# One first stage for a four-layer attention kernel on one Trainium2 core: loads, normalisation and weight folding of layer 0 merged

## The reference, cut to what matters

```
x = x + tanh(g_xattn[0]) * L0_xattn(layernorm(x), ctx, Wq, Wkv_expand, Wout)
# L0_xattn: 16 heads of 16; qp = q @ Wq.T ; k, v = split(ctx @ Wkv.T)
# scores = (qh . kh) / 4, causal, softmax, out = attn . vh, out @ Wout.T
x = x + tanh(g_ffn[0])   * L0_ffn(layernorm(x), ...)          # experts
...
```

## Time and profile before

| what | us |
|---|---|
| median of three runs (lowest, highest) | 2333.84 (2321.99, 2335.94) |
| the profiled execution's own time | 2323.12 |
| its span, first to last instruction | 2321.3 |
| stages load, norma0, fold0: start to first product of q0 | 45.78 |
| q0, its products | 27.09 |
| PE busy over the span | 2176.7 (94%) |
| DVE / ACT / POOL busy | 1479.5 / 923.5 / 1095.1 |
| mean granted TensorE clock | 0.961 |

### The profile page before, as it was taken

One profiled execution on the slowest core, in us unless ns is written; L12 is line 12 of the kernel. 1 busy time (PEld: TensorE's weight loads), 2 busy tenths in 40 slices (PEclk: granted clock), 3 DMA queues, 4 the chain that ended last, 5 costly groups with the idle time before them and its releaser, 6 DMA issues. The chain is left out here.

```text
span 2321.3 us, 38613 instructions
## 1 busy us (share of the span) xinstructions
PE 2176.7 (94%) x13750; PEld 1552.8 (67%) x13750; DVE 1479.5 (64%) x2519; ACT 923.5 (40%) x1430; POOL 1095.1 (47%) x618
## 2 busy tenths in 40 slices
PE   6768999899999998999999999898999999998998
PEld 4447998666665657666666665787565566667997
DVE  2775444477777757787777775413777777744444
ACT  1442444434444452212444444112344444424443
POOL 0330333037777770464777777001077777722332
PEclk7878999999999999999999999899999999998999
DMA  4472732375564513225545552295855545303332
GB/s 84 123 249 94 226 113 90 91 188 111 114 134 105 132 40 127 57 84 127 126 100 137 117 119 49 74 339 226 233 114 123 119 102 133 83 9 111 117 117 83
DMA packets 122054, 285.59 MB, mean 123 GB/s; under 512 B 31355, under 2 KB 73903, under 8 KB 118172
## 3 DMA queue, kind: packets, MB, share of 16 engines
q1 hardware_dynamic: 121244, 281.95, 45.7%
q0 software_dynamic: 672, 1.84, 0.2%
HBM read 237.15 MB, written 46.41 MB: 122 GB/s over the span
## 5 line engine op out<-in xcount | busy, mean ns | idle before, releaser
L1314 DVE TENSOR_REDUCE keep_top<-banks 128x1 f32<-128x500 f32 x945 | 595.6, 674 | 218.5 <-PE banks L1221 218.3
L1391 ACT ACTIVATE att_ex<-banks 125x896 f32<-125x896 f32 x576 | 501.0, 918 | 230.0 <-PE banks L1214 229.9
L1247 PE MATMUL banks<-att_ex,att_v 125*64 125x448 f32 x2304 | 464.7, 545 | 0.0
L1446 POOL TENSOR_TENSOR att_acc<-att_acc,att_ex 125x896 f32<-125x896 f32 x186 | 391.8, 2106 | 68.0 <-ACT att_ex L1391 54.2
L1221 PE MATMUL banks<-keep_kh,keep_qt 64*128 64x500 f32 x1230 | 370.1, 408 | 5.3 <-POOL keep_eye L1429 5.3
L1446 POOL TENSOR_TENSOR att_acc<-att_acc,att_two 125x896 f32<-125x896 f32 x141 | 297.4, 2109 | 164.1 <-DVE att_two L1330 164.1
L1247 PEld LDWEIGHTS banks<-att_ex,att_v 125*64 125x64 f32 x2304 | 152.5, 136 | 247.9 <-issue 207.7
L1214 PE MATMUL banks<-keep_qt,keep_kh 64*125 64x448 f32 x1152 | 309.2, 403 | 7.6 <-ACT att_ex L1391 2.4
L1214 PE MATMUL banks<-keep_qt,att_kl 64*125 64x448 f32 x1152 | 307.5, 363 | 0.0
L1761 PE MATMUL banks<-moe_xs,moe_w 128*128 128x448 f32 x1272 | 282.0, 371 | 4.0 <-DVE moe_w L1857 2.4
L1330 DVE TENSOR_TENSOR att_two<-att_ex 125x896 f32<-125x896 f32 x144 | 244.2, 1696 | 61.2 <-ACT att_ex L1391 58.7
(11 more groups left out here) (291 smaller groups left out, 2678.8 us busy)
## 6 DMA issues: line engine op xcount, KB each, us to landing
keep_kh<-kvt_hi SPq DMA_DIRECT2D x96, 375.0 KB, 5.3
att_kl<-kvt_lo SPq DMA_DIRECT2D x96, 375.0 KB, 7.3
q_rows<-mats_q SPq DMA_DIRECT2D x24, 896.0 KB, 6.1
keep_qt<-q_rows SPq DMA_DIRECT2D x96, 224.0 KB, 6.0
moe_raw<-L_experts_dram SPq DMA_DIRECT2D x53, 384.0 KB
att_v<-kvn SPq DMA_DIRECT2D x24, 720.0 KB
sort_wu<-L_experts_dram SPq DMA_DIRECT2D x14, 1024.0 KB, 9.2
moe_cb<-comb_rows SPq DMA_DIRECT2D x62, 224.0 KB
```

Source lines behind the costliest of these rows:

```text
L1247: last = pe.matmul(PS[WEIGHED][64 * e:64 * e + 64, 0:HALF], v[:, s // 2, u, s % 2, :], ex[:, u % RING, e, :], start=u == 0, stop=u == UNIT ...
L1314: dve.tensor_reduce(top[:, s % 2, n // NS, n % NS:n % NS + 1], PS[MAXIMA + n % 3][:, 0:SB], AX.X, ALU.max).then_inc(mx_done, 1)
L1391: act.activation(ex[:, u % RING], scored, ACT.Exp).then_inc(exp_done, 1)
L1446: pool.tensor_tensor(a, a if n else ex[:, 0], two[:, i] if k == 2 else ex[:, k], ALU.add).then_inc(gathered, 1)
```

## The change

`load_inputs`, the form of `normalise` that loads, and `fold_small` go. One stage, `open_first`, takes the place of the three. It issues the weights ahead of x and the small inputs; the tables move to SP's list in q0. The four weights of layer 0 lie in two lanes: heads 0 to 7 in partitions 0 to 15, heads 8 to 15 in partitions 64 to 79, so that each comes in two DMAs (pieces) instead of one. PE runs 16 products on a zeroed tile first, then the products of A with the two lanes in turn, those of B likewise, and at last the transposes of xn, two tiles of x to a bank. tanh of the gates comes last on ACT.

```diff
-            shapes = {"wq": [HD, NH, H], "wk": [HD, NH, D], "wv": [HD, NH, D], "wo": [HD, NH, H]}
+            shapes = {"wq": [128, HH, H], "wk": [128, HH, D], "wv": [128, HH, D], "wo": [128, HH, H]}
...
+        self.lanes = HD if l == 0 else 0
+            ((0, HH), (HH, NH)) if self.lanes else
...
+        row = a // HH * 64
+        dst = self.tiles[n][row:row + self.lanes, :, :] if self.lanes else self.tiles[n][:, a:z, :]
+        sp.dma_start(dst, self.sources[n][:, a:z, :]).then_inc(self.arrived[n], 16)
...
+HALVES = (0, 2, 1, 3)
+def open_first(nc, G, W, A, Bm):
+            def _(sp):
+                Stage.semaphores.clear_earlier(sp)
+                W.load_one(sp, "wq")
+                W.load_one(sp, "wk")
+                sp.dma_start(x[:, :, :], G["x_in"]).then_inc(x_in, 16)
+                W.load_one(sp, "wv")
+                W.load_one(sp, "wo")
+                sp.dma_start(ident[:, :], G["ident_in"]).then_inc(ident_in, 16)
+                sp.dma_start(G["gate"][:, 0:4], G["g_xattn"].broadcast_to([128, 4])).then_inc(small_in, 16)
+                sp.dma_start(G["gate"][:, 4:8], G["g_ffn"].broadcast_to([128, 4])).then_inc(small_in, 16)
+                sp.wait_ge(zeroed, 2)
+                for u in range(2):
+                    sp.dma_start(k0[64 * u:64 * u + 64, :, S * u:S * u + S],
...
+                    sp.dma_start(v0[64 * u:64 * u + S, :, D * u:D * u + D],
...
+                for dst, src in G["ahead"]:
+                    sp.dma_start(dst, src).then_inc(G["ahead_in"], 16)
+            def _(pool):
+                pool.memset(blank[:, :], 0.0).then_inc(blanked, 1)
+                pool.memset(k0[:, :, :], 0.0).then_inc(zeroed, 1)
+                pool.memset(v0[:, :, :], 0.0).then_inc(zeroed, 1)
+            def _(pe):
+                pe.wait_ge(blanked, 1)
+                for _ in range(16):
+                    pe.matmul(PS[7][:, 0:128], blank[:, :], blank[:, :], start=True, stop=True)
+                W.wait(pe, "wq", "wk")
+                for n in range(2):
+                    for h in range(4 * n, 4 * n + 4):
+                        for k in range(KC):
+                            o = (k * 4 + h % 4) * D
+                            for lane in range(2):
+                                rows = slice(64 * lane, 64 * lane + W.lanes)
+                                last = pe.matmul(PS[n + 2 * lane][:, o:o + D], wq[rows, h, 128 * k:128 * k + 128],
+                                                 wk[rows, h, :], start=True, stop=True)
+                W.wait(pe, "wv", "wo")
+                for n in range(2):
+                    for h in range(4 * n, 4 * n + 4):
+                        o, out = h % 4 // 2 * H, h % 2 * 64
+                        for lane in range(2):
+                            rows = slice(64 * lane, 64 * lane + W.lanes)
+                            last = pe.matmul(PS[4 + n + 2 * lane][out:out + 64, o:o + H], wv[rows, h, :], wo[rows, h, :],
+                                             start=True, stop=True)
+                pe.wait_ge(ident_in, 16)
+                pe.wait_ge(a_done, 4)
+                for i in range(NT):
+                    pe.wait_ge(xn_ready, i + 1)
+                    for k in range(KC):
+                        last = pe.transpose(turned(i)[:, 128 * k:128 * k + 128], xn[:, i, 128 * k:128 * k + 128], ident[:, :])
+                    last.then_inc(tr_done, 1)
+            def _(dve):
+                dve.wait_ge(x_in, 16)
+                for i in range(NT):
+                    c.mark(dve.bn_stats(stats[:, i, :], x[:, i, :]))
...
+                for i in range(NT):
+                    dve.tensor_scalar(xn[:, i, :], x[:, i, :], mv[:, i, 0:1], r[:, i:i + 1],
+                                      ALU.subtract, ALU.mult).then_inc(xn_ready, 1)
+                for n, g in enumerate(HALVES):
+                    dve.wait_ge(b_ready, 2 * (n // 2) + 2)
+                    dve.tensor_copy(Bm[:, 2 * g:2 * g + 2, :],
+                                    PS[4 + g][:, :].rearrange("p (h n) -> p h n", h=2)).then_inc(b_done, 1)
+            def _(act):
+                act.wait_ge(var_ready, 1)
+                act.activation(sd[:, :], ve[:, :], ACT.Sqrt).then_inc(sqrt_done, 1)
+                for n, g in enumerate(HALVES):
+                    act.wait_ge(a_ready, 2 * (n // 2) + 2)
+                    act.activation(A[:, :, 4 * g:4 * g + 4, :],
...
+                for g in range(4):
+                    tiles = min(2, NT - 2 * g)
+                    act.wait_ge(tr_done, 2 * g + tiles)
+                    act.activation(xT[:, :, 256 * g:256 * g + 128 * tiles].rearrange("p k (i n) -> p k i n", i=tiles),
...
+                act.wait_ge(small_in, 96)
+                act.activation(G["tanh"][:, :], G["gate"][:, :], ACT.Tanh).then_inc(tanh_done, 1)
...
                  Stage.semaphores.clear_earlier(sp)
+                for dst, src in G["tables"]:
+                    sp.dma_start(dst, src).then_inc(G["tables_in"], 16)
```

More of the change, by code:

```diff
@@ L133, in keep_running @@
         pe.matmul(bank[:, 0:128], G["ident"][:, :], G["ident"][:, :], start=True, stop=True)
[L136 to L166, removed]
 class Rotation:
@@ L313, in wait, with normalise @@
             pe.wait_ge(self.arrived[n], self.expected[n])
-def normalise(nc, G, name, W=None, stats=None):
+def normalise(nc, G, name, stats):
     x, xT, PS, ident = G["x"], G["xT"], G["PS"], G["ident"]
     with Stage(nc, name) as st:
-        taken, mv = stats is not None, st.sb("mv", [128, NT, 2])
-        if not taken:
-            stats = st.sb("stats", [128, NT, 6])
+        mv = st.sb("mv", [128, NT, 2])
         ve, sd, r, t = (st.sb(n, [128, NT]) for n in ("ve", "sd", "r", "t"))
@@ L331, in _ @@
                 Stage.semaphores.clear_earlier(sp)
[L332 to L337, removed]
             @block.vector
@@ L378, in _, with turned @@
                     last.then_inc(tr_done, 1)
-def fold_small(nc, G, W, A, Bm):
-    PS = G["PS"]
+HALVES = (0, 2, 1, 3)
+def open_first(nc, G, W, A, Bm):
+    PS, x, xn, xT, ident = G["PS"], G["x"], G["xn"], G["xT"], G["ident"]
     wq, wk, wv, wo = (W[n] for n in ("wq", "wk", "wv", "wo"))
-    with Stage(nc, "fold0") as st:
+    k0, v0 = G["k0"], G["v0"]
+    with Stage(nc, "first") as st:
+        blank = st.sb("blank", [128, 128])
+        stats, mv = st.sb("stats", [128, NT, 6]), st.sb("mv", [128, NT, 2])
+        ve, sd, r, t = (st.sb(n, [128, NT]) for n in ("ve", "sd", "r", "t"))
+        blanked, zeroed, x_in, ident_in, small_in, tanh_done = (
+            st.sem(n) for n in ("blanked", "zeroed", "x_in", "ident_in", "small_in", "tanh_done"))
+        chain, var_ready, sqrt_done, xn_ready, tr_done, copied = (
+            st.sem(n) for n in ("chain", "var_ready", "sqrt_done", "xn_ready", "tr_done", "copied"))
         a_ready, b_ready, a_done, b_done = (st.sem(n) for n in ("a_ready", "b_ready", "a_done", "b_done"))
+        def turned(i):
+            return PS[i // 2][:, i % 2 * H:i % 2 * H + H]
         with nc.Block() as block:
@@ L393, in _ @@
+                for dst, src in G["ahead"]:
+                    sp.dma_start(dst, src).then_inc(G["ahead_in"], 16)
+            @block.gpsimd
+            def _(pool):
+                pool.memset(blank[:, :], 0.0).then_inc(blanked, 1)
+                pool.memset(k0[:, :, :], 0.0).then_inc(zeroed, 1)
+                pool.memset(v0[:, :, :], 0.0).then_inc(zeroed, 1)
             @block.tensor
             def _(pe):
-                W.wait(pe)
-                for g in range(4):
-                    for h in range(4 * g, 4 * g + 4):
+                pe.wait_ge(blanked, 1)
[4 more added lines that the diff above has]
+                    for h in range(4 * n, 4 * n + 4):
@@ L398, in _ @@
                         for k in range(KC):
                             o = (k * 4 + h % 4) * D
-                            last = pe.matmul(PS[g][:, o:o + D], wq[:, h, 128 * k:128 * k + 128], wk[:, h, :],
-                                             start=True, stop=True)
[L402 to L408, removed]
+                            for lane in range(2):
+                                rows = slice(64 * lane, 64 * lane + W.lanes)
+                                last = pe.matmul(PS[n + 2 * lane][:, o:o + D], wq[rows, h, 128 * k:128 * k + 128],
+                                                 wk[rows, h, :], start=True, stop=True)
+                                if h % 4 == 3 and k == KC - 1:
+                                    last.then_inc(a_ready, 1)
@@ new lines, in _ @@
+                W.wait(pe, "wv", "wo")
[5 more added lines that the diff above has]
+                            last = pe.matmul(PS[4 + n + 2 * lane][out:out + 64, o:o + H], wv[rows, h, :], wo[rows, h, :],
+                                             start=True, stop=True)
+                            if h % 4 == 3:
+                                last.then_inc(b_ready, 1)
@@ new lines, in _ @@
+                pe.wait_ge(ident_in, 16)
```

(22 more changed lines are left out.)

23 lines of the change are left out of this document (6 added, 17 removed).

## The result

Four runs of the changed kernel have a median of 2302.9 us (2297.73 to 2304.42), beside 2330.45 for the kernel before (2321.99 to 2335.94, four runs: the three of the table above and one more). The ratio is 0.9887, with a 95% interval from 0.9867 to 0.9906: faster by 1.1%, some 26 us. The forecast was 2308, in a range from 2293 to 2319.

A forecast was written before the change was run, and what follows sets the result against it. PE bounds the kernel, so only the opening can pay: q0 starting at 22.9 instead of 45.8 us gains 22.9, q0's clock 2.9, together 25.8. From the median 2333.8 that gives 2308; the range is 2293 to 2319.

The forecast's parts named there:

- A's first product: Start of the fold on PE: weights land at 6.9 us, the 16 blank products over by about 5 and free.
- A and B: Fold on PE: overlapping lanes at 1.2 GHz bring A to 6.9 us and B to 3.5, ending at 17.4.
- rival 1: Fold: blank products hold the clock up, transposes end about 15.3, gain 31.1 us, time 2303; chance 12%.
- x off the path: Opening: x lands by 10.4 us, xn done by 17.1, just before the transposes can start at 17.4.
- Transposes to q0: End of the opening: transposes to 20.6, last copy 21.0, table load and tanh to 22.5, q0 starts at 22.9 us.
- q0's clock: q0 on PE: full clock from the start after the transposes, 24.2 us instead of 27.09, a gain of 2.9.
- Rival 3: q0 starts at 1.2 GHz, by the idle gap or the rule on transposes; time 2311 us, chance 12%.
- SP and the tables: SP's queue: first stage's issues done at about 12 us; nine tables take 8.5 us beside q0, costing nothing.
- att0 and the rest: Behind q0: the rest of the trace shifts by 26 us with the same lengths.
- rival 5: att0, behind q0: PE's short bursts catch the low clock throughout, 6 us slower, 2340; chance 3%.

The follow-up runs named there:

- no_blank: The changed kernel without the 16 blank products on PE; median 2304.43 us, ratio 0.9871 to the kernel before.
- lanes_apart: The changed kernel with all of one lane's heads first, then the other's, within each half of A, and B's loops turned likewise; median 2304.29 us, ratio 0.9864.
- tables_first: The changed kernel with the nine tables issued at the end of the first stage instead of in q0; median 2305.18 us, ratio 0.9866 to the kernel before.
- again: The changed kernel, nothing altered, run and profiled a second time; median 2304.11 us, ratio 0.9872 to the kernel before.
- third: The changed kernel, nothing altered, run and profiled a third time; median 2303.92 us, ratio 0.9896 to the kernel before.
- x_first: The changed kernel with x issued ahead of wq and wk instead of behind them; median 2305.14 us, ratio 0.990 to the kernel before.
- held: The changed kernel with tanh moved to att0, two copies of A ahead of the square root, two blank products behind the transposes; median 2299.33 us, ratio 0.9856.
- best: held with a square root of one blank column as ACT's first instruction; median 2297.71 us, ratio 0.9866 to the kernel before.
- old_again: The kernel before, nothing altered, run and profiled a second time; median 2330.1 us, ratio 0.9993, span 2331.2 us.

## Why the prediction was right, and where its steps were not

The forecast of 25.8 us stands against 27.8 in the opening's trace and some 26 by the ratio. The sum was right, while several of its terms were wrong, and that these errors cancelled is luck: nothing in the prediction ties one to the other. The forecast time, 2308, lies 5 us above the measured 2302.9; 3.4 of these come from the median that the gain was taken from (2333.84 of three runs, 2330.45 with the fourth).

- **A's first product**: forecast 6.9, measured 6.87, for another reason. The weights land at 5.1 (no_blank), and the blank products, which I had as free and over by 5, hold PE until 6.9. I had priced them by the transposes; a blank product is two instructions.
- **A and B**: I took 6.9 and 3.5 us. no_blank measures 7.09 and 3.69, so these terms fit at 1.2 GHz, and for A lanes_apart bears out the mechanism of the lanes, read from layer 1's fold; for B it doesn't show it. The changed kernel took 3.79 and 2.11. The step that failed is the clock: I gave rival 1 (the blank products hold it up) 12%, on the ground that 21 us of 16-row products had never raised it. They don't raise it, but it fell under them only at about 12.3. In tables_first it fell at 10.3 already, so 3.79 and 2.11 are not fixed prices either.
- **x off the path**: wrong. With the fold over at 12.7 instead of 17.4, the transposes waited until 13.48 for ACT, which copies A only behind the square root and so behind x (the row of PE's transposes in the changed profile names `mats_A`). Rival 1 had the transposes end at 15.3; measured 16.7. With x at 8.12 the forecast's own 4.9 us to the first tile of xn and 3.25 of transposes give 16.3, so rival 1 was priced too low; the rest is ACT's copies.
- **Transposes to q0**: forecast 5.5 us from start to q0 (17.4 to 22.9), measured 5.5 (13.48 to 19.01), with 1.28 for the table load right behind the copy (16.31 + 0.87 = 17.18, load at 17.20). The drain of which the Trainium skill speaks (ScalarE: Activation LUTs, What ACT_TABLE_LOAD costs) is not there: tanh starts at 18.50, 0.02 us behind the load's end.
- **q0's clock**: I took 2.9 us for a full clock from the first product. Measured 1.1 in the changed kernel, -0.2 in again, 1.1 in third. Rival 3, to which I gave 12%, is what happened in the first profile and in again, and nearly so in third, where q0 started at 1.00 and lost it after 0.6 us; lanes_apart, x_first, held and best had the whole 2.8. The Trainium skill (TensorE: Matmul & The Clock Gate, Part 4) would have it that transposes don't count. held and third show the clock rising while they run (at about 16.2 and 15.9), so that rule is not the reason. The reason stays open: in the three profiles of the changed kernel, with the same instructions on PE, the clock came up again at about 22.5, 24.9 and 15.9.
- **SP and the tables**: no cost, as forecast; nine issues in q0 took 4.1 us (19.86 to 24.00). SP was done at 14.2 instead of 12.
- **att0 and the rest** (rival 5): no loss was found beyond what executions of one kernel differ by. From q0's end to ACT's next table load behind att0's head it is 100.9 to 102.3 us in the three profiles of the old code, and 100.8 to 103.5 in the seven of the new.

So what happened in the changed kernel's first profile is rivals 1 and 3 together: 3.9 us more before q0 than forecast, 1.8 us less in it.

## What to carry to other kernels

A stage ends with the last engine, and a queue that only issues DMAs is one of them: look for the stretch in which all engines are idle while one still issues, and move those issues into a stage that is bound elsewhere. A short stage's cost depends on the clock that it inherits, so price each of its terms at both levels, ask what ran before it, and profile the same kernel more than once before a difference of 2 us is put down to an edit. Changes of 5 us and less in a kernel of 2300 us are read from the trace at the marks around them, not from medians whose runs lie 7 to 20 us apart.

## What was not expected of the hardware

- The granted clock's column said 1.00 for products that ran at half the pace (no_blank), until the first change in the trace.
- Two-lane products of 16 rows kept the full clock for a while after dense work (5.4 us from A's first product in the changed kernel, 2.7 in tables_first), but in the profile before, products of 16 rows did not raise it in 21 us.
- A load of the table for tanh also served the exponentials of att0: the changed kernel has no table load at att0's head, where the kernel before had one at 73.8.
- PE can stand still for 2 us and more with nothing to wait for in the profile, in one execution and not in another; the stage in which it did so in old_again was 5.9 us longer.
